# Forming the second layer's angle differences on GpSimd, in three buffers, instead of on VectorE in two

## What is computed

```
qp = [sin(p), cos(p)] / 4,   p = R @ unit(rope(q))        16 query heads, 8 random directions
kp = [sin(p), cos(p)] / 4,   the same of k                 8 key heads
kv = einsum('bhsf,bhsd->bsfd', kp, v)
out = einsum('bhsf,bsfd->bhsd', qp, kv)                    then out @ Wo.T + bo
```

## Time and profile before

| what | value |
|---|---|
| time, median of 3 runs | 533.49 us (528.59 to 534.28) |
| time of the profiled execution | 531.84 us |
| its span | 530.0 us |
| its mean granted PE clock | 0.983 |
| busy: PE, DVE, ACT, POOL | 492.1, 357.5, 299.6, 303.5 us |

### The profile page before, as it was taken

One profiled execution on the slowest core, in us unless ns is written; L12 is line 12 of the kernel. 1 busy time (PEld: TensorE's weight loads), 2 busy tenths in 40 slices (PEclk: granted clock), 3 DMA queues, 4 the chain that ended last, 5 costly groups with the idle time before them and its releaser, 6 DMA issues. The chain is left out here.

```text
span 530.0 us, 9787 instructions
## 1 busy us (share of the span) xinstructions
PE 492.1 (93%) x2935; PEld 356.9 (67%) x2935; DVE 357.5 (67%) x1030; ACT 299.6 (57%) x667; POOL 303.5 (57%) x231
## 2 busy tenths in 40 slices
PE   8999799989799999999999999999979979899982
PEld 7666676778577777778777778786665535466661
DVE  6999735847767475576484681615477979999645
ACT  1256076687685776765766756747312358466530
POOL 1046447887877678576686786744133065788440
PEclk9999799999899999999999999999999999999998
DMA  7991738999779978588686796863669021444437
GB/s 222 330 365 36 206 100 190 201 205 276 185 172 287 223 169 193 100 192 191 133 209 136 151 228 151 186 111 31 171 200 309 15 69 61 99 117 108 86 81 236
DMA packets 92996, 89.20 MB, mean 168 GB/s; under 512 B 28273, under 2 KB 87793, under 8 KB 92561
## 3 DMA queue, kind: packets, MB, share of 16 engines
q1 hardware_dynamic: 73440, 59.25, 38.9%
q0 software_dynamic: 17376, 27.24, 27.2%
q10 hardware_dynamic: 2128, 2.10, 1.2%
HBM read 65.42 MB, written 21.29 MB: 164 GB/s over the span
## 5 line engine op out<-in xcount | busy, mean ns | idle before, releaser
L987 POOL DMA_INDIRECT expert_sums<-expert_weights,token_of_slot x79 | 131.5, 1665 | 60.8 <-ACT expert_weights L1097 32.7
L979 POOL DMA_INDIRECT expert_weights<-normed_x,token_of_slot x79 | 91.1, 1153 | 40.2 <-issue 17.9
L581 PE MATMUL bank<-out_weights,expert_weights 128*128 128x256 f32 x256 | 60.2, 381 | 0.7 <-ACT expert_weights L707 0.7
L581 PEld LDWEIGHTS bank<-out_weights,expert_weights 128*128 128x128 f32 x256 | 46.5, 190 | 8.0 <-ACT expert_weights L707 1.8
L1021 PEld LDWEIGHTS bank<-expert_weights 128*128 128x128 f32 x316 | 39.4, 191 | 11.1 <-issue 7.9
L1021 PE MATMUL bank<-expert_weights 128*128 128x128 f32 x316 | 43.8, 281 | 2.6 <-DMA expert_weights<-experts_in 2.0
L1320 PE MATMUL bank<-expert_weights,tiles 128*128 x92 | 44.1, 602 | 1.3 <-DVE tiles L1370 1.3
L1284 POOL DMA_INDIRECT tiles<-normed_x,token_of_slot x23 | 27.5, 1194 | 29.8 <-DVE token_of_slot L1278 20.5
L1043 PE MATMUL bank<-expert_weights 128*128 128x256 f32 x158 | 43.2, 392 | 0.7 <-ACT expert_weights L1074 0.7
L820 DVE SCALAR_TENSOR_TENSOR expert_weights<-bank,blocks_valid 128x64 f32<-128x64 f32 x32 | 7.2, 224 | 50.3 <-ACT expert_weights L684 49.1
L1289 POOL DMA_INDIRECT expert_rows<-expert_weights,token_of_slot x23 | 30.1, 1311 | 18.9 <-ACT expert_weights L1365 14.3
(11 more groups left out here) (282 smaller groups left out, 1124.5 us busy)
## 6 DMA issues: line engine op xcount, KB each, us to landing
expert_weights<-experts_in SPq DMA_DIRECT2D x79, 177.5 KB
expert_weights<-experts_out SPq DMA_DIRECT2D x79, 128.0 KB
expert_weights<-experts_rest SPq DMA_DIRECT2D x79, 64.2 KB
expert_weights<-L_ffn_wi SPq DMA_DIRECT2D x32, 128.0 KB
expert_weights<-w_comp SPq DMA_DIRECT2D x1, 2048.0 KB, 12.0
expert_weights<-fold_g SPq DMA_DIRECT2D x1, 2048.0 KB, 15.1
expert_sums<-zeros SPq DMA_DIRECT2D x2, 1024.0 KB, 21.1
expert_weights<-L_ffn_wo SPq DMA_DIRECT2D x16, 128.0 KB
```

What stands on the lines that cost most here:

```text
L581: ins = nc.tensor.matmul(ps[7][:, 0:HID], AO[:, h * P:(h + 1) * P], wc3[:, h, :], start=(h == 0), stop=(h == H - 1))
L979: nc.gpsimd.indirect_dma_start(xt0[g % 4], None, xn0, bass.IndirectOffsetOnAxis(ap=MAP[:, g:g + 1], axis=0)).then_inc(gathered[g % 4], 16)
L987: nc.gpsimd.indirect_dma_start(sums0[g % 2], bass.IndirectOffsetOnAxis(ap=MAP[:, g:g + 1], axis=0), yt0[g % 4], None, compute_op=ALU.add). ...
```

## The change

The differences of all eight tiles move from DVE to POOL. POOL forms those of tile 0 in its beat 0, of tile 1 in beat 1, of tile 2 in beat 2, of tile 3 in beat 5, and then of one tile every three beats: 4 in beat 8, 5 in 11, 6 in 14, 7 in 17, each behind the gather and the write of that beat. There are three buffers in place of two; the third lies in `PBS`, whose first half was last used by the turned queries of layer 1. POOL waits for `U`, for `meet` of tile t - 3 to be over (t >= 3), and at t = 2 for the angles to have been taken.

```diff
+APART1 = {0: 0, 1: 1, **{3 * t - 4: t for t in range(2, NT)}}
...
-        DIFF = [YG[:, i * NPH:(i + 1) * NPH] for i in range(2)]
+        DIFF = [YG[:, 0:NPH], YG[:, NPH:2 * NPH], PBS[:, 0:NPH]]
...
-        def differences(dve, t):
+        def differences(pool, t):
             u = v3(U, NT * NHK)[:, t * NHK:(t + 1) * NHK, :]
-            dve.wait_ge(u_ok, t // 2 + 1)
-            nc.vector.tensor_tensor(DIFF[t % 2].rearrange("p (h k e) -> p h k e", h=H1, k=HKV),
+            pool.wait_ge(u_ok, t // 2 + 1)
+            if t >= 3:
+                pool.wait_ge(o_ok, t - 2)
+            elif t == 2:
+                pool.wait_ge(at_sb, 4)
+            nc.gpsimd.tensor_tensor(DIFF[t % 3].rearrange("p (h k e) -> p h k e", h=H1, k=HKV),
                                     bc(u[:, 0:H1].unsqueeze(2), [P, H1, HKV, R1]),
                                     bc(u[:, H1:].unsqueeze(1), [P, H1, HKV, R1]), ALU.subtract).then_inc(apart, 1)
...
             turns(dve, st, 0)
-            differences(dve, 0)
             turns(dve, st, 1)
             for t in range(NT):
-                if t + 1 < NT:
-                    differences(dve, t + 1)
                 if t == NT - 2:
                     middle(dve, 3 * t)
...
                     if i >= 5:
                         write_tile1(pool, i - 5)
+                    if i in APART1:
+                        differences(pool, APART1[i])
```

More of the change, by code:

```diff
@@ L1417, in sines_of @@
             act.wait_ge(apart, t + 1)
-            nc.scalar.activation(DIFF[t % 2], DIFF[t % 2], ACT.Sin, scale=3.1415925).then_inc(sines, 1)
+            nc.scalar.activation(DIFF[t % 3], DIFF[t % 3], ACT.Sin, scale=3.1415925).then_inc(sines, 1)
         def squares_of(act, t):
             act.wait_ge(sines, t + 1)
-            nc.scalar.activation(DIFF[t % 2], DIFF[t % 2], ACT.Square).then_inc(squared, 1)
+            nc.scalar.activation(DIFF[t % 3], DIFF[t % 3], ACT.Square).then_inc(squared, 1)
         def meet(dve, st, t, part):
@@ L1429, in meet @@
                 dve.wait_ge(squared, t + 1)
-                st.link(nc.vector.tensor_reduce(w, DIFF[t % 2].rearrange("p (h k e) -> p h k e", h=H1, k=HKV), AX, ALU.add))
+                st.link(nc.vector.tensor_reduce(w, DIFF[t % 3].rearrange("p (h k e) -> p h k e", h=H1, k=HKV), AX, ALU.add))
                 st.link(nc.vector.tensor_scalar(w, w, -4.0 / D1, float(R1 * 2) / D1, ALU.mult, ALU.add))
```

## The result

The changed kernel takes 544.48 us (median of 4 runs, 541.63 to 547.13) against 533.88 us for the kernel before (4 runs, 528.59 to 535.97). The ratio is 1.0214, with a 95% interval of 1.0164 to 1.0263: slower by 2.1%. The forecast was +1.4%, 541.0 us. In every ratio of this text, executions that took over 1.5% more than the fastest one of their kernel are left out as slow.

The account below looks back on a forecast made before the run. The prediction took DVE's chain to bound the pipeline until 457 us, then PE, with POOL bounding after the change. 0 (start) + 7.4 (POOL late) + 0 (tail) on 531.84 gave 539.2, plus 1.65 to the median: 541.0 us; range 533.0 to 547.5.

Parts of the forecast that it names:

- POOL as the bound: Layer 1's pipeline: POOL, given the differences, falls behind PE's beats and sets the pace, 11.5 us against 9.06 per three beats.
- start 0: Pipeline start to PE's beat 10: sines 2.0 to 2.3 us later, DVE's chain saves 2.28 us; the two cancel.
- POOL late 7.4: Last gather (tile 22) lands at 502.9 us against PE's earlier transpose at 495.45, so PE is 7.4 us late.
- tail 0: Projection, loads and last sums behind the pipeline keep their length, as POOL catches up before the end: 0 us.
- collisions: POOL's DMA issues lengthened by DVE products: 1.5 us for each of six plus 1.0 for shorter ones, 10.0 us together.
- idle waits: POOL's waits for others before 460 us, part of 8 us in the kernel before, vanish once POOL itself is late.
- The landing: A gather's data reaches PE about 2.45 us behind the end of its issue on POOL.
- the one on the lock: A POOL difference may hold a DVE `meet` product up to 2.2 us; hidden behind POOL, so 0.
- Faster: Rival: POOL forms a difference in DVE's 1.2 us; about -1.1 us, 532.4 us; chance of slightly faster 0.10.
- No change: Rival: differences take 2.2 us but products seldom hit a POOL issue; gathers land in time, 533.5 us; chance 0.16.
- Slower by more: Rival: broadcast views make a POOL difference 3.2 us; 15.4 us late, 549 us; POOL later than 12 us, chance 0.12.
- What was to be seen: Signs: POOL nearly without idle, PE waiting for gathers, tile 7's sines about 500 us, longer beats from 16, products over 4 us.

Follow-up runs that it names:

- f3: Only tile 0's difference on POOL, tiles 1 to 7 on DVE, three buffers, against the kernel before: ratio 1.0137; tile 22 +2.38 us.
- e1: Differences of tiles 0 to 3 on POOL, tiles 4 to 7 on DVE, against the kernel before: ratio 1.0072; tile 22 +5.06 us.
- f1: Kernel before, differences on DVE, plus two unread gathers on POOL in each of the eight places: ratio 1.0258; tile 22 +12.85 us.
- g1: Differences of tiles 2 to 7 on POOL, tiles 0 and 1 on DVE, against the kernel before: ratio 1.0106; tile 22 +5.25 us.
- f2: Differences of tiles 5, 6 and 7 on POOL, tiles 0 to 4 on DVE, against the kernel before: ratio 1.0111; tile 22 +3.62 us.
- e2: Differences of tiles 4 to 7 on POOL, tiles 0 to 3 on DVE, against the kernel before: ratio 1.0134; tile 22 +6.64 us.
- e3: Kernel before, differences on DVE, plus an unread POOL memset in each of the eight places: ratio 1.0138; tile 22 +11.72 us.
- f4: Kernel before with a third buffer alone, all differences on DVE in the old order: ratio 1.0065; tile 22 -0.03 us.

## Why the prediction was right, and where it wasn't

**POOL as the bound: right.** The sum was start 0, POOL late 7.4, tail 0. By its terms: the issues are as they were; a difference was put at 2.2 and took 2.35 to 2.39 us, but the gaps around it are 0.02 and 0.16 us where I had taken 0.1 and 0.3, so 2.24 net for 2.3; collisions cost 10.4 us for 10.0; idle waits 1.1 us for 0. The stretch from the first gather was put at 500.4 - 425.94 = 74.5 us and is 75.35. The landing was put at 2.45 us and took 3.46 (503.58 to 507.04). Hence 0.9 + 1.0 on 7.4: 9.3 us. The terms that were mis-sized are POOL's idle waits (0 for 1.1 us, partly made good by the shorter differences) and the landing (2.45 for 3.46 us), which I took from one early gather in a quiet stretch. The profiled execution was forecast at 539.2 us and took 543.44: 1.9 us of that miss are these two, and 2.3 us lie ahead of the pipeline, where nothing was changed.

**The start: wrong, at 0.** The step said that at beat 10 the late sines and the saved differences cancel, and the one on the lock said that a held product is hidden behind POOL. Tile 11 was late by 6.09 us. The late sines cost 2.37 (ACT's first sine 9.24 us behind the first gather in place of 6.87), the held instructions 2.29 + 2.29 + 1.36, less 2.28 saved: 6.03. I had set a hold's price in the stage where PE is the chain, and not in the stage where DVE is, though the prediction itself had named that stage. f3 shows the first term alone (+2.38), e1 the most of them together (+5.06).

**Why the sum was near all the same.** The two delays lie side by side, and the end takes the later: POOL, without pause from the first gather on, is late by itself at the end (f1: 0.11 at tile 11, 8.59 at tile 21, ahead of the wait of ACT that is not shown to be POOL's), so the 6.1 us of the start are covered by its 9.3. At most the 1.1 us of idle waits in its stretch can stem from the start. That this is a maximum is shown by POOL's missing idle time rather than by a run that takes the start's delay away and nothing else; g1 comes near to one, and came out between the two readings. That the wrong term cost nothing is luck: in e1, where POOL has half of the differences, the forecast of no change in the start misses by 5 us, the whole of the delay, and in the changed kernel 3.2 us less of POOL's time (9.3 less 6.1, an estimate) would have been enough for that.

**The rivals.** *Faster* needed a difference of 1.2 us; it takes 2.36. *No change* needed products that miss POOL's issues: in the stretch six issues took over 1.8 us, and all 36 together took 10.4 us more than 0.98 us each. *Slower by more* needed 3.2 us for broadcast views; 2.31 ns a number is close to the 2.2 of the plain row of 2048. On what speaks for these collisions against the Trainium skill, "SBUF — State Buffer", section "Who interferes with whom" (a DVE tensor_tensor wouldn't stall descriptor generation): the gather at 444.59 took 2.84 us and ended 0.83 us behind the product that ran to 446.60. The trace disagrees, in every kernel of this study (five or six issues of over 1.8 us in each stretch).

**What was to be seen.** Right: POOL without idle time, PE's waits for gathers (tile 20, 0.95 us at 499.12, and tile 22, 1.63 at 507.04; I had named 16, 19 and 22), the product of over 4 us. The sines of tile 0 came 2.4 us later (2.0 to 2.3 forecast), those of tile 7 began at 502.80 (about 500 forecast, in a trace whose pipeline starts 2.3 us later), and PE's beats lengthened only from beat 19, where I had said 16. Not foreseen: PE's clock. After 3.17 us without work, waiting for ACT behind the sines, its next four matmuls took 3.40 us (granted clock 0.52 from 440 to 443 us). DVE's held product hid it in the changed kernel.

## What to carry to other kernels

Count what POOL is occupied with, not what the profile calls busy: from one indirect DMA to the next 0.30 us pass here that no row counts (only 0.02 us from an issue to a difference, 0.16 us from there to the next issue), and 57% busy over the span was 86% occupied in the one stage that mattered. Before an elementwise operation goes to POOL, look for what DVE does at that moment with two SBUF inputs or a scaling from SBUF to SBUF, as it stood still here until POOL's instruction was over, for up to 2.8 us (a product of the norms in g1, 3.01 us for 0.26); in a stage where DVE sets the pace, each such meeting is paid in full. An idle wait of the engine that owned the work may be the better place: the same differences, moved 1 to 2 tiles ahead on DVE, gave a gain of 1.5 us where POOL gave a loss of 9.3.

## What the runs showed of the hardware that I had not expected

A GpSimd memset of 2250 columns (1.99 us) held DVE's scalings, 2.77 us in place of 0.23, and not the instructions with two inputs (2.28 and 1.22 us as ever). Which of the two engines comes first can't be read from the starts of the rows: the held instructions of f2, e2 and e3 began 0.38, 0.39 and 0.70 us ahead of POOL's row.

PE's clock: waits of 3.17, 3.18, 3.24, 3.39 and 3.47 us were each followed by a stretch at or near the lower level of 1.2 GHz (granted clock 0.50 to 0.52, four matmuls in 3.1 to 3.8 us in place of 1.98), one of 3.13 us (f3) wasn't. Nor does the length of the wait alone divide them: behind one of 2.80 us in f1 four matmuls of L1340 took 2.02 us in place of 1.03 (granted clock 0.59 from 509.0 to 511.3 us). The slow stretch comes on top of the wait: 1.5 us in e2.

Two programs with the same beats (f4 and the kernel before) differed by 0.65% (0.24 to 1.06%) in whole time, 0.47% by the medians of all executions. What goes with it is PE's granted clock: the kernel before took 529.73 us at a mean of 0.990 and 544.76 at 0.971 on that chip, and the mean was 0.980 over f4's ten executions and 0.9845 over the nineteen of the kernel before. Why it was lower is open; no run here was made for it.
